# Four graph networks in one kernel: another setup, one-hots shared with ScalarE, an output stage that signals by groups

## Time and profile before

| | us |
|---|---|
| median of 3 runs | 6075.76 (6075.24 to 6083.95) |
| the profiled execution | 6077.61 |
| its span | 6075.9 |
| DVE busy | 4149.0 (68%) |
| POOL busy | 4107.5 (68%) |
| PE busy | 3771.4 (62%) |
| ACT busy | 2325.5 (38%) |

### The profile page before, as it was taken

One profiled execution on the slowest core, in us unless ns is written; L12 is line 12 of the kernel. 1 busy time (PEld: TensorE's weight loads), 2 busy tenths in 40 slices (PEclk: granted clock), 3 DMA queues, 4 the chain that ended last, 5 costly groups with the idle time before them and its releaser, 6 DMA issues. The chain is left out here.

```text
span 6075.9 us, 77367 instructions
## 1 busy us (share of the span) xinstructions
PE 3771.4 (62%) x19710; PEld 2555.2 (42%) x19710; DVE 4149.0 (68%) x14950; ACT 2325.5 (38%) x6170; POOL 4107.5 (68%) x4026
## 2 busy tenths in 40 slices
PE   2777788888558878886777455467747736660000
PEld 1444455555335545554555344356635523330000
DVE  6999799999744434443555566566669967885554
ACT  0000377777611111112555576522215548980000
POOL 5777777777767767776776677577730057774776
PEclk9999999999755555555566566577768878895555
DMA  1111344333223333333454355423325547762221
GB/s 40 48 48 48 103 149 152 132 116 111 98 67 98 100 91 98 98 98 111 147 162 143 114 157 155 146 86 97 97 71 218 218 119 147 154 144 74 100 92 66
DMA packets 413662, 685.60 MB, mean 113 GB/s; under 512 B 283685, under 2 KB 290444, under 8 KB 407978
## 3 DMA queue, kind: packets, MB, share of 16 engines
q1 hardware_dynamic: 282410, 542.14, 25.3%
q0 software_dynamic: 130944, 140.05, 12.6%
HBM read 310.94 MB, written 373.78 MB: 113 GB/s over the span
## 5 line engine op out<-in xcount | busy, mean ns | idle before, releaser
L778 POOL DMA_INDIRECT G<-states,srcq x1568 | 1583.5, 1010 | 489.9 <-issue 476.5
L1884 PE MATMUL PS<-ident,HH 128*128 128x128 f32 x2357 | 519.0, 364 | 734.6 <-DVE HH L1372 321.8
L1465 DVE SCALAR_TENSOR_TENSOR R<-R,same,G 128x64 f32<-128x64 f32 x1568 | 448.1, 286 | 695.9 <-DMA G<-states,srcq 579.5
L2174 ACT COPY AT<-PS 128x512 f32<-128x512 f32 (+1 forms) x494 | 284.8, 582 | 1312.6 <-PE PS L1899 829.9
L1884 PEld LDWEIGHTS PS<-ident,HH 128*128 128x128 f32 x2357 | 367.6, 189 | 896.1 <-DVE HH L1372 353.6
L1899 PEld LDWEIGHTS PS<-WD,AT 128*128 128x128 f32 x2358 | 486.1, 305 | 174.6 <-issue 174.3
L1899 PE MATMUL PS<-WD,AT 128*128 128x64 f32 x2358 | 539.8, 404 | 0.0
L891 POOL DMA_INDIRECT out_nodes<-O,dstq x392 | 396.2, 1011 | 190.9 <-issue 123.4
L778 POOL DMA_INDIRECT EE<-node_info,srcq x392 | 411.4, 1050 | 134.2 <-issue 134.2
L778 POOL DMA_INDIRECT PG<-in_x,dsti x392 | 407.4, 1039 | 119.9 <-issue 119.5
L778 POOL DMA_INDIRECT G<-states,srci x392 | 404.7, 1032 | 119.4 <-issue 117.9
(11 more groups left out here) (451 smaller groups left out, 10073.1 us busy)
## 6 DMA issues: line engine op xcount, KB each, us to landing
states<-O SPq DMA_DIRECT2D x70, 896.0 KB, 3.6
HH<-states SPq DMA_DIRECT2D x56, 896.0 KB
total<-R SPq DMA_DIRECT2D x56, 896.0 KB, 3.6
XB<-resid SPq DMA_DIRECT2D x42, 896.0 KB, 6.4
states<-HH SPq DMA_DIRECT2D x28, 896.0 KB, 5.0
G<-states,srcq POOLq DMA_INDIRECT x1568, 2.5
resid<-XB SPq DMA_DIRECT2D x28, 896.0 KB, 6.9
xl_of_src<-O SPq DMA_DIRECT2D x14, 1792.0 KB, 6.9
```

The costliest lines, as they stand in the source:

```text
L778: return pool.indirect_dma_start(to, None, table_, bass.IndirectOffsetOnAxis(ap=idx, axis=0), bounds_check=bound, oob_is_err=False).then_i ...
L1465: row = dve.scalar_tensor_tensor(out=R[:, b, j * D:(j + 1) * D], in0=row_before, scalar=same[:, bass.ds(i * C + j, 1)], in1=G[:, b, j * D: ...
L1884: last = pe.transpose(PS[:, 4 + k, q * P:(q + 1) * P], HH[:, b, (g * G4 + q) * D2:(g * G4 + q + 1) * D2], ident[:])
L2174: act.copy(AT[:, k, 0:n * P], PS[:, 4 + k, 0:n * P]).then_inc(s_copied, 1)
```

## The change

Six edits, in three stages.

1. Setup, loads: each index tensor is loaded as 112, 15 and 1 rows; `dst` has a semaphore of its own, `s_dst`. SP waits for 3 fills, not 6. The 34 weight loads stand, unchanged, in ScalarE's program.
2. Setup, order check: DVE no longer clears `HH` and `R` and waits for `dst` alone. Three products on PE with the identity turn the last column, the first column and the column of maxima into rows of PSUM; DVE compares them on one partition. POOL's four DMAs are gone. The wait for all six other index loads stands before `s_order`.
3. Bins: ACT makes the `256`-wide one-hots by `relu(1 - |f - iota|)`, all four of the first kind and two of the four of the second; DVE makes the 392-wide ones and the two that are left.
4. x rows: turns 2 to 21 are stored by SP, between its setup barrier and its wait for the bins.
5. sum2 on DVE: per group of 4 columns, weight, four row sums with a column's flag (`scalar_tensor_tensor`) and output, with a signal for each group; POOL waits for each group. A chunk's buffers are guarded by waits of DVE on stores and scatters.
6. sum2 on SP: the sums are stored as soon as DVE is done, and the next loads issued behind, with no wait for scatters; those are awaited once, at the end.

```diff
-            sp.wait_ge(s_fill, 6)
-            for to, of in ((dsti, dst), (srci, src), (tmp[:].bitcast(I32), etype)):
-                sp.dma_start(to[0:FULL, :], ...).then_inc(s_in, 16)
-                sp.dma_start(to[FULL:P, 0:REST], ...).then_inc(s_in, 16)
+            EVEN = FULL // 16 * 16
+            sp.wait_ge(s_fill, 3)
+            for to, of, loaded in ((dsti, dst, s_dst), (srci, src, s_in), (tmp[:].bitcast(I32), etype, s_in)):
+                for first, end in ((0, EVEN), (EVEN, FULL)):
+                    sp.dma_start(to[first:end, :], ...).then_inc(loaded, 16)
+                sp.dma_start(to[FULL:P, 0:REST], ...).then_inc(loaded, 16)
...
+            for turn in SP_KEEPS:                      # range(2, 22)
+                b = turn % 2
+                sp.wait_ge(s_pg[b], 16 * PC * (turn // 2 + 1))
+                sp.dma_start(chunk(xsrc, turn, PC * D), PG[:, b, :]).then_inc(s_pst_sp[b], 16)
             sp.wait_ge(s_bins, 1)
...
+            def totals(i, it, b, more=True):           # sum2, SP
+                sp.wait_ge(s_ready, before["sum2", "ready"] + GROUPS * (i + 1))
+                sp.dma_start(chunk(total_g2, i, CD), R[:, b, 0:CD]).then_inc(s_st[b], 16)
+                if more:
+                    load_weighted(i + 2, b)
...
-            pool.wait_ge(s_asked, 1)                   # setup, POOL
-            move(sort_line, few[:, 0:1])
-            move(few[1:P, 1:2], sort_line[0:P - 1])
...
-                pool.wait_ge(s_ready, before["sum2", "ready"] + 1 + i)
                 for j in range(C):
+                    if j % G4 == 0:
+                        pool.wait_ge(s_ready, before["sum2", "ready"] + GROUPS * i + j // G4 + 1)
                     scatter(O[:, b, j * D:(j + 1) * D], out, ...)
...
-            step(dve.memset(HH[:], 0.0))               # setup, DVE
-            step(dve.memset(R[:], 0.0))
-            dve.wait_ge(s_in, 16 * 6)
+            dve.wait_ge(s_dst, 16 * 3)
             step(cast(number, dsti[:]))
             step(dve.memset(few[:], -1.0))
             step(tt(one[:, 1:], number[:, 0:TILES - 1], number[:, 1:], ALU.is_gt))
+            step(dve.memset(one[:, 0:1], 0.0))
+            dve.tensor_reduce(few[:, 0:1], one, AX_X, ALU.max).then_inc(s_ends, 1)
+            dve.wait_ge(s_met, 1)
+            step(cast(ends, PS[0:1, 7, 0:P]))
+            step(dve.memset(out_of_order, 0.0))
+            step(tt(out_of_order[:, 1:], ends[:, 0:P - 1], PS[0:1, 7, P + 1:2 * P], ALU.is_gt))
+            step(tt(out_of_order, out_of_order, PS[0:1, 7, 2 * P:3 * P], ALU.max))
+            step(dve.tensor_reduce(few[0:1, 2:3], out_of_order, AX_X, ALU.max))
+            cast(few[0:1, 3:4].bitcast(I32), few[0:1, 2:3]).then_inc(s_asked, 1)
...
+            dve.wait_ge(s_in, 16 * 6)
             dve.drain().then_inc(s_order, 1)
...
+            def weighted2(i, it, b, first=False):      # sum2, DVE
+                step.reset()
+                dve.wait_ge(s_ld[b], before["sum2", "ld"] + 32 * (it + 1))
+                if not first:
+                    dve.wait_ge(s_st[b], before["sum2", "st"] + 16 * it)
+                    dve.wait_ge(s_sc[b], it * (16 * C))
+                step(dve.memset(col(SCR), 0.0))
+                for g in range(GROUPS):
+                    rows_, at = slice(g * G4 * D, (g + 1) * G4 * D), bass.ds(i * C + g * G4, G4)
+                    some = cut(G[:, b, rows_])
+                    step(tt(some, some, over(Eb[:, 0, at], D), ALU.mult))
+                    for j in range(g * G4, (g + 1) * G4):
+                        row_before = R[:, b, (j - 1) * D:j * D] if j else R[:, 1 - b, CD - D:CD]
+                        step(dve.scalar_tensor_tensor(out=R[:, b, j * D:(j + 1) * D], in0=row_before, scalar=same[:, ...],
+                                                      in1=G[:, b, j * D:(j + 1) * D], op0=ALU.mult, op1=ALU.add))
+                    result(R[:, b, rows_], O[:, b, rows_], XB[:, b, rows_], G4, over(Ec[:, 0, at], D)).then_inc(s_ready, 1)
...
+            for k, ends in enumerate((number[:, TILES - 1:TILES], number[:, 0:1], few[:, 0:1])):   # setup, PE
+                last = pe.matmul(PS[0:1, 7, k * P:(k + 1) * P], ends, ident[:], start=True, stop=True)
+            last.then_inc(s_met, 1)
...
+            for to, of in loads:                       # setup, ACT: the 34 weight loads
+                act.dma_start(to, of).then_inc(s_w, 16)
...
+            with act.Fori(0, HTURNS) as it:            # bins, ACT
+                for b in range(2):
+                    act.wait_ge(s_fields, 2 * it + b + 1)
+                    for k in range(HCOLS):
+                        last = act.activation(hot[:, k, low:low + 256], iota_h[:, 0:256], ACT.Abs, bias=fw[:, b, 1, k:k + 1], scale=-1.0)
+                        if k < HCOLS // 2:
+                            last = act.activation(hot[:, k, low + 256:low + 512], iota_h[:, 0:256], ACT.Abs, bias=fw[:, b, 3, k:k + 1], scale=-1.0)
+                    last.then_inc(s_far, 1)
+                    act.wait_ge(s_far, 2 * it + b + 1)
+                    act.activation(both, both, ACT.Relu, bias=onec[:], scale=-1.0)    # 2 x 512 columns
+                    act.activation(one_, one_, ACT.Relu, bias=onec[:], scale=-1.0).then_inc(s_hot_low, 1)    # 2 x 256
```

More of the change, by code:

```diff
@@ L358, in build_program, with kept_rows @@
         FEATS_AT_ONCE = 8
+        SP_KEEPS = range(2, 22)
+        def kept_rows(turn):
+            by_sp = turn in SP_KEEPS
+            return (s_pst_sp if by_sp else s_pst)[turn % 2], 16 * sum((at in SP_KEEPS) == by_sp for at in range(turn % 2, turn + 1, 2))
         HOT_COLS = 7
@@ L456, in _ @@
[L456 to L470, removed]
+            EVEN = FULL // 16 * 16
+            sp.wait_ge(s_fill, 3)
+            for to, of, loaded in ((dsti, dst, s_dst), (srci, src, s_in), (tmp[:].bitcast(I32), etype, s_in)):
+                for first, end in ((0, EVEN), (EVEN, FULL)):
+                    sp.dma_start(to[first:end, :], of[first * TILES:end * TILES].rearrange("(p t) -> p t", t=TILES)).then_inc(loaded, 16)
+                sp.dma_start(to[FULL:P, 0:REST], of[FULL * TILES:E].rearrange("(p t) -> p t", p=1)).then_inc(loaded, 16)
@@ L541, in _ @@
             barrier()
[L543 to L564, removed]
             def products_out(phase):
@@ L740, in _, with load_weighted @@
             barrier()
[L742 to L748, removed]
+            def load_weighted(i, b):
+                for to, of in ((G, xl2), (XB, resid[2])):
+                    sp.dma_start(to[:, b, :], chunk(of, i, CD)).then_inc(s_ld[b], 16)
+            def totals(i, it, b, more=True):
[4 more added lines that the diff above has]
+            for b in range(2):
+                load_weighted(b, b)
+            paired(sp, TURNS - 1, totals)
+            for b in range(2):
+                totals(CHUNKS - 2 + b, TURNS - 1, b, more=False)
+            for b in range(2):
+                sp.wait_ge(s_st[b], before["sum2", "st"] + 16 * TURNS)
+                sp.wait_ge(s_sc[b], 16 * C * TURNS)
             barrier()
@@ L857, in _ @@
                 if turn >= 2:
-                    pool.wait_ge(s_pst[b], 16 * (turn // 2))
+                    pool.wait_ge(*kept_rows(turn - 2))
                 for j in range(PC):
@@ L861, in _ @@
                     gather(PG[:, b, j * D:(j + 1) * D], x, idx[:, at:at + 1], N - 1, s_pg[b])
-                    if j == PC // 2 and turn:
+                    if j == PC // 2 and turn and turn - 1 not in SP_KEEPS:
                         keep_rows(turn - 1)
@@ L1729, in result @@
                 return by_parts(cut(o), cut(o), cut(xb), ALU.add)
[L1731 removed]
+            def weighted2(i, it, b, first=False):
                 step.reset()
                 dve.wait_ge(s_ld[b], before["sum2", "ld"] + 32 * (it + 1))
[L1734 to L1740 removed]
+                if not first:
[8 more added lines that the diff above has]
+                        row_before = R[:, b, (j - 1) * D:j * D] if j else R[:, 1 - b, CD - D:CD]
+                        step(dve.scalar_tensor_tensor(out=R[:, b, j * D:(j + 1) * D], in0=row_before, scalar=same[:, bass.ds(i * C + j, 1)],
+                                                      in1=G[:, b, j * D:(j + 1) * D], op0=ALU.mult, op1=ALU.add))
+                    result(R[:, b, rows_], O[:, b, rows_], XB[:, b, rows_], G4, over(Ec[:, 0, at], D)).then_inc(s_ready, 1)
+            for b in range(2):
+                weighted2(b, 0, b, first=True)
+            paired(dve, TURNS, weighted2, start=1)
             step.reset()
```

89 lines of the change are left out of this document (43 added, 46 removed).

## The result

The change makes the kernel faster: 5995.98 us (median of 4 runs, 5992.33 to 6007.77) against 6075.5 us, ratio 0.9872 with a 95% interval from 0.9858 to 0.9887. In two later comparisons, again with the kernel before on the same chip, the ratios were 0.9886 [0.9871, 0.9901] and 0.9864 [0.9842, 0.9885]. By medians the gain is 71 to 80 us; 77.6 was forecast. The profiled execution of the changed kernel happens to be the longest of its four, 6007.8 us with a span of 6006.0, 69.9 shorter than the span before. Single executions of one kernel differ by 5 to 36 us here, so small terms are read from stretches of several traces.

A forecast was written before the change was run, and what follows sets the result against it. POOL was taken as the path up to prep and in the last stage; 44.2 + 12 + 17.9 + 3.5 = 77.6 off the profiled 6077.6 gives 6000.0, by the median of runs 5998, range 5985 to 6020.

The forecast's parts named there:

- POOL is the path up to prep, with 26 us to spare for the edges: From 0 to 1693 us POOL alone is the path; the edge stage's DVE looks like the bound but has 26 us spare.
- forecast of prep at 1637: End of the edge stage: DVE's prep still released by POOL, at about 1637, with the edges' last store about 80 before.
- Setup, 44.2: Edits 1 and 2: first gather at 16.5 instead of 60.7, gain 44.2 us, bounds 30 and 47.
- Rival A: Setup: index loads come late, rows not spread or weights in their way; setup gains 30, total 6012; chance 13%.
- Stores, 12: Edit 4: 20 stores taken off POOL at 0.59 each save 12 us, bounds 0 and 20.
- Bins, nothing on the path: Edit 3: bins shrink by 70 us (30 to 110), worth nothing on the path because POOL is last already.
- rival C: Bins: `Abs` and `Relu` table loads make 7.3 us a batch, 170 lost, 6168, slower than before; chance 4%.
- rival B: Edge stage arrives last as ACT sets bins at 5.6 to 6.2 us a batch; at 6.0, 43 lost, 6041; chance 8%.
- `x_of_dst` as what comes next late: After the bins, the first chunk of `x_of_dst` is what comes next late, with 39 us of spare left.
- Last stage, 17.9 + 3.5: Edits 5 and 6: first scatter gains 17.9 us, tail barrier opens about 3.5 earlier; together 21.4, bounds 14 and 25.
- No pause between groups: Last stage: scatters at 1.33 us each, with POOL never waiting again after the first group.
- Nothing between prep and the last stage: Between edge and last stage, code and waits are the same and barriers pass the shift on in full; put at nothing.

The follow-up runs named there:

- the slowed bins: Two more 1024-wide activations of 1.06 us a batch on ScalarE, added to the changed kernel's bins: 6062.03 us, 58 above the changed kernel.

## Why the prediction was right

- **POOL is the path up to prep, with 26 us to spare for the edges.** Right: in every kernel whose bins kept pace POOL releases prep, and only the slowed bins changed that. The forecast of prep at 1637, 56 earlier, was too early: it starts at 1648.65, 1641.15 and 1650.76 in the three traces of the changed kernel, 43 to 52 earlier, since the row of gathers gave 0.8, 8.5 and -1.2 against the one trace before and not 12. The edges' last store is issued 115 to 124 before prep, not 80. Without edit 3 the spare is 29 and not 14: what was left out is that bins fed by VectorE alone shorten by 12 when SP takes the stores.
- **Setup, 44.2.** Right: first gather at 16.64 where 16.5 was summed, so 44.1, and 40 by the medians of the kernel with it alone. By parts: DVE's start of the check 7.04 (6.9), PE's word 10.48 (10.7), last cast over at 12.11 (12.3), from there 4.53 (4.18). Rival A, loads late, did not occur; with 127 rows it does, at 12 us where 14 was its price.
- **Stores, 12.** POOL issues 36 stores after (8 by `src`, 28 by `dst`), 56 before. Right in size, as far as the scatter lets one tell: 10.2 by the traces of thirteen executions, 11.7 and 12.6 by medians.
- **Bins, nothing on the path.** Right: with edit 3 undone the time is the same. Its own forecast of 4.7 a batch (4.2 to 5.1) came to 4.5. ScalarE's groups after, from 60 to 505 us:

```profile
L2072 ACT ACTIVATE R<-iota_h,fw 128x256 f16<-128x256 f16 x391 | 184.8, 496 | 21.3 <-DVE fw L1129 19.4
L2078 ACT ACTIVATE R<-R,onec 128x1024 f16<-128x1024 f16 x98 | 112.5, 1148 | 3.2
L2074 ACT ACTIVATE R<-iota_h,fw 128x256 f16<-128x256 f16 x196 | 96.5, 492 | 0.0
L2079 ACT ACTIVATE R<-R,onec 128x512 f16<-128x512 f16 x98 | 69.2, 706 | 0.0
```

  No table load stands among the bins' groups, so rival C fails at its condition. The Trainium skill, "ScalarE: Activation LUTs", section "Table sets: the hidden batching unit", has abs and relu in every set; the trace agrees, with no load in 98 batches. At 4.5 a batch rival B's point of 5.56 is not reached either; the slowed bins, at 6.3, show that B's mechanism is real once it is passed.
- **`x_of_dst` as what comes next late.** Not reached, but nearer than summed: the first chunk's load stands at 608.8 and its second store at about 572.2 + 19 = 591 plus landing of 3.4 (median after), a spare of 14 instead of 39: the bins gave 91 and not 70 (21), and POOL's store came 51 earlier and not 56 (5).
- **Last stage, 17.9 + 3.5.** Right: 18.3 and 3.5, and a first group of 3.2 us where 3.6 was summed (four row sums took 1.25, in layer 0 1.57). "No pause between groups" was wrong in the letter: POOL is released by DVE 15 times in the stage, the first after 54.45 us, the patch's scatter after 3.40, and the 13 between in 0.3 us, its usual gap.
- **Nothing between prep and the last stage.** Right to the noise: from the first layer gather to the first loads of the last stage are 3789.5 us before (1718.8 to 5508.3) and 3788.0 after (1674.0 to 5462.0).

The parts add up: 40 (setup) + 12.6 (stores) + 18 (last stage) = 70.6 by medians, where all together gave 71 in the same group. Each part is sure to some 7 us or worse, so that they agree to 1 is partly luck. So is the first median's 5995.98, 2 below the forecast's 5998: the later medians of the same kernel are 6003.85 and 6000.91, and the gain of 77.6 lies between 71 and 80. The mechanisms were right, and the sum a few microseconds high.

## What to carry to other kernels

On a seam, ask who arrives last and by how much: 91 us of faster bins were worth nothing, and one earlier start of an engine with a fixed row of 1176 gathers was worth 40 by medians, 44 by its trace. Count the instructions that the bounding engine issues for others (20 stores, 10 to 12 us) and the small round trips through DRAM before its first useful one (24.6 us of check brought to 5.1, first gather 19 earlier). A stage that a bounding engine ends should be fed by the smallest piece that keeps it busy, here a group of 4 scatters (5.3 us) made in 3.2.

## What the runs showed of the hardware that I had not expected

- The executions of one program differ by more than the smaller terms of this sum: 5984.0 to 6011.7 in five runs of the changed kernel. Part of it is in POOL's own row of gathers: 1615.1 to 1624.8 us for the same 1176 gathers. POOL pauses there at times although the profile shows nothing that it waits for, here for 5.71 us, and twice more for 3.2 among the `node_info` gathers (the kernel before has three of 3.2 to 3.7); the timeline of POOL in the changed kernel:

```profile
1250.97 1.62 POOL L766 DMA_INDIRECT EE<-node_info,srcq  x1 [0.31 <-issue]
1258.31 1.00 POOL L766 DMA_INDIRECT EE<-node_info,srcq  x1 [5.71 <-issue]
```

  What it waits for was not tried.
- A store of one 4-byte number for each of 128 partitions (512 bytes) from POOL took 6.60 and 7.50 us after its issue with the check by POOL, more than two index loads of 196 KB with 128 rows need to land (2.8 us).
